# ALiBi attention scores over 128 zero-padded rows, value projections beside the first moves, and head moves from two queues

## The reference

```python
qkv = clip(einsum('bsd,ed->bse', x, w_qkv), -8, 8)
q, k, v = split(qkv, 3)
q = layer_norm(q, q_ln_w, q_ln_b); k = layer_norm(k, k_ln_w, k_ln_b)
# 32 heads of 16
scores = einsum('bqhd,bkhd->bhqk', q, k) * 0.25 + slope[h] * (key_pos - query_pos)
probs = softmax(where(key_pos <= query_pos, scores, -inf))
attn = einsum('bhqk,bkhd->bqhd', probs, v)
```

## Time and profile before

| what | value |
|---|---|
| time, median of 3 runs | 1611.9 us (1610.43 to 1612.72) |
| profiled execution | 1604.95 us, span 1603.1 us |
| PE busy | 1452.5 us, 91% of the span |
| DVE / ACT / POOL busy | 57% / 50% / 31% |
| mean granted TensorE clock | 0.943 of full |
| DMA | 75.37 MB |
| stage_alibi | about 952 to 1323 us |

### The profile page before, as it was taken

How to read it: one execution, slowest core, us unless ns; L and a number is a source line. 1 busy time by engine, 2 the same in 40 slices (tenths; PEclk the granted TensorE clock), 3 DMA queues, 4 the chain that set the end, 5 groups by cost and what they waited for, 6 DMA issues and landing times. The chain is left out here.

```text
span 1603.1 us, 25066 instructions
## 1 busy us (share of the span) xinstructions
PE 1452.5 (91%) x8832; PEld 1009.4 (63%) x8832; DVE 908.2 (57%) x1375; ACT 795.0 (50%) x1723; POOL 500.1 (31%) x413
## 2 busy tenths in 40 slices
PE   5499999999999999999858974789899899999996
PEld 4367667666776676667636862445455437888885
DVE  4145445455554554555556864666666506867976
ACT  2366555655665555666513310355566555433343
POOL 0444433334444333344034440000000004444442
PEclk9699999999999999999969995699999969999999
DMA  3244544444445434443540028033343205000000
GB/s 119 48 48 48 51 35 46 47 40 40 44 47 50 35 46 48 38 39 37 81 90 1 1 30 117 12 55 54 55 55 55 87 1 223 0 1 0 1 27 27
DMA packets 46614, 75.37 MB, mean 47 GB/s; under 512 B 18640, under 2 KB 24912, under 8 KB 45392
## 3 DMA queue, kind: packets, MB, share of 16 engines
q1 hardware_dynamic: 45376, 70.04, 31.2%
q0 software_dynamic: 1168, 4.39, 2.1%
HBM read 41.82 MB, written 2.10 MB: 27 GB/s over the span
## 5 line engine op out<-in xcount | busy, mean ns | idle before, releaser
L674 DVE TENSOR_REDUCE nmax<-sc 128x1 f32<-128x128 f32 (+7 forms) x256 | 192.5, 752 | 181.8 <-PE sc L462 181.8
L1491 ACT ACTIVATE l_probs<-l_banks 128x512 f32<-128x512 f32 (+3 forms) x384 | 165.8, 495 | 157.3 <-PE l_banks L1434 122.5
L605 ACT COPY pt<-tb 128x512 f32<-128x512 f32 (+3 forms) x256 | 129.3, 505 | 201.4 <-PE tb L476 199.8
L1520 DVE TENSOR_REDUCE pm<-l_sm 128x2 f32<-128x1024 f32 (+1 forms) x192 | 176.0, 955 | 93.2 <-PE l_sm L1405 51.3
L597 ACT ACTIVATE probs<-sc,nmax 128x128 f32<-128x128 f32 (+7 forms) x256 | 190.6, 745 | 56.6 <-DVE nmax L674 56.4
L476 PE MATMUL tb<-ident,probs 128*128 128x128 f32 x1152 | 174.2, 276 | 2.0 <-ACT pt L605 1.1
L78 PE MATMUL sc<-k_h,q_h 128*128 128x512 f32 (+3 forms) x384 | 144.7, 377 | 22.1 <-POOL q_l L745 14.5
L1405 PE MATMUL l_sm<-kT,qT 64*128 64x512 f32 (+3 forms) x384 | 112.8, 463 | 46.8 <-DMA kT<-late 24.3
L1430 PE MATMUL l_banks<-qT,kT 64*128 64x512 f32 (+3 forms) x384 | 137.5, 461 | 14.6 <-DMA qT<-mT 11.3
L500 PE MATMUL mb<-pt,ckv 128*64 128x512 f32 (+3 forms) x768 | 137.7, 494 | 0.1
L78 PE MATMUL sc<-k_l,q_h 128*128 128x512 f32 (+3 forms) x384 | 133.7, 348 | 0.0
(11 more groups left out here) (266 smaller groups left out, 3125.6 us busy)
## 6 DMA issues: line engine op xcount, KB each, us to landing
gated_late<-in_gated SPq DMA_DIRECT2D x11, 768.0 KB, 14.4
wout<-in_w_out SPq DMA_DIRECT2D x16, 512.0 KB, 7.1
late<-late SPq DMA_DIRECT2D x128, 64.0 KB, 2.0
rb<-rT SPq DMA_DIRECT2D x64, 128.0 KB, 8.8
qT<-late SPq DMA_DIRECT2D x96, 64.0 KB, 4.3
nope_t<-in_nope_by_dim SPq DMA_DIRECT2D x16, 192.0 KB, 5.6
kT<-late SPq DMA_DIRECT2D x48, 64.0 KB, 3.6
kT<-stage SPq DMA_DIRECT2D x48, 64.0 KB, 2.9
```

Source lines behind the costliest of these rows:

```text
L605: act.copy(pt[i // 4][:, e, j0:j0 + nb, (i % 4) * P:(i % 4 + 1) * P], tb[TB[g]][:, 0:nb, :]).then_inc(pt_act, 1)
L674: dve.tensor_reduce(nmax[:, n % 4:n % 4 + 1], sc[n % 2][:, 0:(n // 2 + 1) * P], AX.X, ALU.max, negate=True).then_inc(negmax, 1)
L1491: act.activation(probs[(NC * g + c) % RING][:, h, 0:w], banks[:, (E_STEPS * g + n) % SLOTS, 0:w], ACT.Exp).then_inc(exped, 1)
L1520: dve.tensor_reduce(pm[g % 2][:, 2 * s:2 * s + 2, i, half], slot(("m", g, n))[:, :, 0:w], AX.X, ALU.max, negate=True).then_inc(freed, 1)
```

## The change

- The v projections leave `stage_front` and become steps ("v", 0, j) of `alibi_order`: four after the first build, four among the first eight m units. They write the e banks, ACT copies them to `keep.v`, and the clip of v is done by POOL when it fills `vx`.
- The norm weights and biases come as one [128, 4, 4] tile; a build's DVE step multiplies and adds them per partition while it takes the turned block out of PSUM. `scale_q` and its counterpart for k on POOL are gone. ACT then makes the high part from SBUF, and POOL (DVE in the first build) the low part.
- `keys(b, h)` is now one 128-row tile per head, zero in the other head's 64 rows, and `queries(b, s)` holds two heads. So m and e contract over 128 rows, and one bf16 mask matmul of 128 rows takes the place of two of 64.
- SP moves the queries, POOL the keys. The maxima go in four DMAs instead of eight.
- One staging area instead of two; chunks 1, 2 and 3 are built in groups 0, 2 and 4. x and the v weights lie in the buffers of groups 1 and 2, which are filled only when the v projections are done (`vp`).

```diff
@@ alibi_order
-    order = [("build", 0, 0), ("build", 0, 1)]
-    order += [("m", 0, n) for n in range(2)] + [("build", 1, 0), ("build", 1, 1)]
-    order += [("m", 0, n) for n in range(2, NM)] + [("top", 0, 0), ("m", 1, 0), ("rows", 0, 0)]
+    order = [("build", 0, 0), ("build", 0, 1)] + [("v", 0, j) for j in range(4)]
+    for n in range(NM):
+        order.append(("m", 0, n))
+        if n % 2 == 1 and n // 2 < 4:
+            order.append(("v", 0, 4 + n // 2))
+    order += [("top", 0, 0), ("m", 1, 0), ("rows", 0, 0)]
...
-        if g in (1, 3):
-            ahead[8:8] = [("build", (g + 3) // 2, 0)]
-            ahead[12:12] = [("build", (g + 3) // 2, 1)]
+        if g % 2 == 0 and g // 2 + 1 < GROUPS // 2:
+            ahead[2:2] = [("build", g // 2 + 1, 0)]
+            ahead[5:5] = [("build", g // 2 + 1, 1)]
@@ moves and maxima
+        def move(eng, g, which, landed):
+            b = g % BUFS
+            for h in range(HG):
+                src = slice(KR * (g % 2) + HD1 * h, KR * (g % 2) + HD1 * (h + 1))
+                dst, parts = ((queries(b, h // 2), (0, 0, 1)), (keys(b, h), (2, 3, 2)))[which]
+                for n, w in enumerate(parts):
+                    r0 = KR * (h % 2) + EX + HD1 * n
+                    eng.dma_start(dst[r0:r0 + HD1, :].bitcast(F32), stages[w][src, :]).then_inc(landed[b], 16)
...
+                sp.wait_ge(low, 1)
+                move(sp, 0, 0, moved)
+                sp.wait_ge(vp, ST)
+                move(sp, 1, 0, moved)
                 maxima(0)
@@ tensor: m and e
-                        r = half_rows(par)
-                        last = pe.matmul(dst[:, par, 0:w], qT[b][r, s, i * P:(i + 1) * P], kT[b][r, s, c0:c0 + w],
+                        last = pe.matmul(dst[:, par, 0:w], queries(b, s)[:, i * P:(i + 1) * P], keys(b, 2 * s + par)[:, c0:c0 + w],
                                          start=True, stop=not diagonal)
-                    if diagonal:
-                        for z in range(2):
-                            for par in range(2):
-                                r = half_rows(par)
-                                last = pe.matmul(dst[:, par, w - P:w], ident2[r, z, :], mask_m[r, z, :], start=False, stop=z == 1)
+                        if diagonal:
+                            last = pe.matmul(dst[:, par, w - P:w], keep.ident_b[:], keep.mask[:], start=False, stop=True)
@@ scalar, vector: build
-                    act.wait_ge(turned, 2 * chunk + which + 1)
-                    act.copy(stage(chunk, 2 * which).bitcast(F32R),
-                             slot(("build", chunk, which))[:].rearrange("p b c -> p (b c)")).then_inc(high, 1)
+                    act.wait_ge(freed, uses["build", chunk, which] + 1)
+                    act.copy(stages[2 * which].bitcast(F32R), stages[2 * which + 1]).then_inc(high, 1)
...
-                    dve.wait_ge(high, 2 * chunk + which + 1)
-                    dve.tensor_tensor(stage(chunk, 2 * which + 1).bitcast(F32R),
-                                      slot(("build", chunk, which))[:].rearrange("p b c -> p (b c)"),
-                                      stage(chunk, 2 * which), ALU.subtract).then_inc(freed, 1)
+                    dve.wait_ge(turned, 2 * chunk + which + 1)
+                    w, b = (keep.ln[:, 2 * which + n, chunk:chunk + 1] for n in range(2))
+                    dve.tensor_scalar(stages[2 * which + 1], flat_slot(("build", chunk, which)), w, b, ALU.mult, ALU.add).then_inc(freed, 1)
@@ gpsimd
+                pads(0)
+                load_rows(0)
+                move_keys(0)
...
+                pool.wait_ge(vp, ST)
+                for b in range(1, BUFS):
+                    pads(b)
+                    load_rows(b)
+                    if b == 1:
+                        move_keys(1)
...
+                    if g % 2 == 0 and g // 2 + 1 < GROUPS // 2:
+                        lower(g // 2 + 1, 0)
+                        lower(g // 2 + 1, 1)
                     if g + 2 < GROUPS:
-                        load_rows(g + 2)
-                    pool.wait_ge(pv_ps, NC * g)
-                    values(g + 1, (g + 1) % 2)
+                        move_keys(g + 2)
```

More of the change, by code:

```diff
@@ L832, in stage_front @@
         names = ("tr_ps tr_h tr_l w_h w_l x_late ag_ps ag_ev back_ps score masked biased out_ps out_ev wqh wql "
[L833 removed]
+                 "qkv_ps clip")
         (tr_ps, tr_h, tr_l, w_h, w_l, x_late, ag_ps, ag_ev, back_ps, score, masked, biased, out_ps, out_ev,
[L835 removed]
+         wqh, wql, qkv_ps, clip) = (al.sem("c_" + n) for n in names.split())
         ON_ACT = (6, 7)
         LO, X2 = ST, ST + 2
[L838 to L839 removed]
+        order = [(j, c) for j in range(ST) for c in range(2)]
+        dest = (keep.q, keep.k)
         def cols(j):
@@ L991, in qkv_copy @@
                     for k in ks:
-                        part = slice(c * D, (c + 1) * D)
-                        act.copy(wq_h[:, k, part], raw_qkv[c][:, k, :]).then_inc(wqh, 1)
+                        act.copy(wqkv_h[c][:, k, :], raw_qkv[c][:, k, :]).then_inc(wqh, 1)
                 def normalise(j):
@@ L1219, in alibi_rows @@
     return q, k
-def half_masks():
-    r, c = np.arange(P)[:, None] % KR, np.arange(P)[None, :]
-    out = np.zeros((P, 6, P), np.float32)
-    for b in range(2):
-        row = r + KR * b
-        out[:, b], out[:, 2 + b], out[:, 4 + b] = c == row, np.where(c > row, NEG, 0.0), np.where(row > c, NEG, 0.0)
-    return out
 CHUNKS = [(j, half) for half in range(2) for j in range(4 * (half + 1))]
@@ L1343, in _ @@
             def _(sp):
-                def move(g):
-                    chunk, b = g // 2, g % BUFS
-                    sp.wait_ge(freed, uses["build", chunk, 1] + 1)
-                    if g >= BUFS:
-                        sp.wait_ge(sE, E_STEPS * (g - BUFS + 1))
-                    for h in range(HG):
-                        src = slice(KR * (g % 2) + HD1 * h, KR * (g % 2) + HD1 * (h + 1))
-                        for dst, which in ((qT[b], (0, 0, 1)), (kT[b], (2, 3, 2))):
-                            for n, w in enumerate(which):
-                                r0 = KR * (h % 2) + EX + HD1 * n
-                                sp.dma_start(dst[r0:r0 + HD1, h // 2, :].bitcast(F32),
-                                             stage(chunk, w)[src, :]).then_inc(moved[b], 16)
@@ L1555, in _ @@
                         build(g, n)
+                        if g == 0 and n == 1:
+                            lower(0)
+                            lower(1)
                     elif kind == "m":
@@ L1572, in values, with lower, move_keys @@
+                def lower(chunk, which):
+                    pool.wait_ge(high, 2 * chunk + which + 1)
+                    pool.tensor_tensor(stages[2 * which + 1].bitcast(F32R), stages[2 * which + 1], stages[2 * which],
+                                       ALU.subtract).then_inc(low, 1)
+                def move_keys(g):
+                    pool.wait_ge(low, 2 * (g // 2) + 2)
+                    move(pool, g, 1, alibi_in)
                 def values(g, u):
-                    pool.tensor_copy(vx[u][:, :, :, 0:HD1], cols(keep.v, g)).then_inc(vx_ok, 1)
```

241 lines of the change are left out of this document (128 added, 113 removed).

## The result

| | before | after |
|---|---|---|
| median of the runs, us | 1612.31 (1610.43 to 1614.37, 4 runs) | 1588.26 (1584.82 to 1589.39, 4 runs) |
| profiled execution, us | 1604.95 | 1588.67 |
| its span, us | 1603.1 | 1586.8 |

The changed kernel takes 0.9847 of the time before (95% interval 0.9827 to 0.9867). It is faster, as forecast, but by 24 us where 47 were forecast, and 1588.26 is 1.3 us above the range. The two traces differ by 16.3 us of span; the rest of the 24 is mostly that the profiled execution of before was 7 us under its own median. What follows explains the 16.3.

The account below looks back on a forecast made before the run. PE was taken to bound the steady groups, and the DMA moves of group 0 the stage's start. Terms of 24 + 12 + 11 = 47 us, taken from the 1611.9 median, gave 1565 us; range 1551 to 1587.

Parts of the forecast that it names:

- Term A: Start of the ALiBi stage: first exponent score at 993 instead of 1017.3 us; 24 us gained, 17 to 28 by its bounds.
- rival 4: Start of the stage: the second queue gains nothing, group 0 lands at 962, group 1 as much later; 1575 us, chance 0.13.
- Term B: Groups 0 to 6: steady groups take 35 us, groups 1 and 3 fall to 35; 12 us gained, bounds -17 to 21.
- the sum of PE's work over 128 rows: One group: scores 17.8, masks 4.5, values 8.9, transposes and changes of shape 2.2; 33.4 us of work.
- the case with all waits kept: Steady group if PE's waits all stay: 36.2 us, against 33.4 with none and 35 taken.
- rival 3: Scores: packing was fully used before, so a group takes 43.4 us instead of 35; 1624 us, chance 0.04.
- Builds: Groups that turn the next columns (0, 2 and 4): 16 transposes, 1.8 us, and a little waiting; 2.3 us more.
- Rival 1: Groups: DVE and ACT hold slots as now, more narrow shapes wait for weights; 37.4 us a group, 1582, chance 0.18.
- Term C: Last group: shorter wait and fuller array keep the clock near full, 29 us instead of 40.4; 11 us gained.

## Why the prediction was wrong

- **Term A** (24 forecast, 19.2 measured, of which 2.0 are luck ahead of the stage and 17.2 the change's) was right but for one step. The first score stands at 956.0, forecast 955. Group 1's came at 990.8 instead of 986: v's last block ended 3.5 us later than 970, since PE's clock was 0.75 there, and POOL clears 3.65 us before it issues. The exponent scores followed 7.3 us behind, forecast 7. The run with one queue gives the second queue 6.6 us, so rival 4, by which it gains nothing, did not come.
- **Term B** is where it failed: 12 us forecast, -14.2 measured. The step is the sum of PE's work over 128 rows, 33.4 us. PE was busy 37.8 in the steady groups. The rate of the earlier trace rows, 0.23, is that of a 512-column matmul between others like it. 64 of the 96 scores have a mask beside them. For the 48 of 256 columns and more, score and mask take 0.05 more than priced (0.35 for 512 columns instead of 0.30), 2.4 us a group; for the 16 of 128 columns the price was right. Scores beside the 12 value blocks take about 0.1 more on either side, again 2.4 us a group, against which the sum had about 1.3 for changes of shape (its 2.2 less 0.9 for the transposes). I did not vary that alone. The rest is in the value blocks, 9.4 us instead of 8.9, and in rounding. The waits that I took off the group before were 2.1 in it and not 2.8; that bears on the case with all waits kept (36.2) and not on the 33.4. The earlier trace rows could not show it, as the mask there stood before a matmul of 128 columns, and I took its 0.07 as its whole price.
- In the same term I took 0.5 us a group as the cost of giving up row packing, and called the case that packing had been used (rival 3) nearly excluded, because 33.4 was a sum of work. The sum was what was wrong. Packing had been worth 4.4 us a group, half of the 8.9 of that rival: the rule of the Trainium skill ("TensorEngine Tiling (Array Packing)", section "Theoretical Speedup") was right in sign, and "up to twice" is far from what this stream gets.
- Builds: 3.9 us over a steady group, forecast 2.3. DVE no longer waits for ACT in a build, as forecast; the 1.8 us of transposes are there, and PE's waits for DVE and ACT rise from 0.6 to 1.9 us (group at 1158.7); 0.8 us I did not trace.
- **Rival 1** named 37.4 a group and a time of 1582, close to what came, but for the wrong reason: waits fell from 2.1 to 0.6 us. Its clause on narrow shapes, that they cost more than their columns, was the true part; that it is their weights they wait for is likely, not shown.
- **Term C** (11 forecast, 12.0 measured) held: 27.5 us at a clock of 1.00. I gave the shorter wait and the fuller array as its causes together; the runs separate them. With the long wait and full rows the group takes 30.5, with the short wait and half rows 38.1, so most of the gain is the full rows'.

So the traces show the forecast with seven groups 3 to 5 us longer each: 17 us of the 47. That the medians differ by 24 is owed to the 7 us by which the execution that was read for the forecast lay under its median, and without them the miss would have been larger. The range failed on the same point: the upper bound of Term B was thought of as waits that stay, which are counted from what is seen, and not as work that I had never seen in this sequence.

## What to carry to other kernels

A matmul's price is from its start to the next one's start in the sequence in which it will stand. Where wide and short ones alternate, price the pair, with a floor for the short one (here 0.12 us with a score behind it), and look for rows of that very sequence; a rate read in a uniform run is only a lower bound. When a part is taken out to learn its price, look at the waits that come in its place. Where two forms of the same work differ in rate and in how they keep the clock, choose by stretch: here packed rows where PE is bound by its queue, and full rows in the one stretch that follows a wait with little work.

## What was not expected of the hardware

- The last group's scores over 64 rows, with half masks, stayed at half clock for 27 us (0.64 of 38.1) behind a wait of 1.1 us; over 128 rows, behind the same wait, they never left full clock (last groups of 38.1 and 27.5 us).
- Mixing 64-row and 128-row matmuls is slower than either alone: 39.2 us against 34.0 and 38.4, at about 0.2 us for each turn.
- A mask of 384 or 512 columns instead of 128 costs about half of its added columns: 2.7 us of 5.1; one of 256 costs nothing more.
- fp32r weights for a mask cost nothing against bf16, though their load is recorded at 0.19 instead of 0.10 us (38.4 us a group either way, with a score ahead of each mask).
